# Softmax sums through GpSimd: four key tiles of probabilities added first, values in four column groups

## The reference, cut to what matters

```
x = _group_norm(input, gn_weight, gn_bias)
qkv = jnp.einsum('bchw,oc->bohw', x, qkv_weight)          # q, k, v: 4 heads x 32 channels
attn = jnp.einsum('bnchw,bncyx->bnhwyx', q, k) / math.sqrt(C)
attn = jax.nn.softmax(attn.reshape(B, N_HEAD, H, W, H * W), axis=-1)
out = jnp.einsum('bnhwyx,bncyx->bnchw', attn, v)
out = jnp.einsum('bchw,oc->bohw', out, out_weight) + out_bias[:, None, None]
return out + input
```

## Time and profile before

| | |
|---|---|
| median of 3 runs | 394.5 us (392.34 to 397.24) |
| the profiled execution, its own time | 393.55 us |
| its span, first to last instruction | 391.8 us |
| mean granted clock of PE | 0.916 of full speed |
| busy: PE, DVE, ACT, POOL | 326.7, 222.2, 187.9, 112.0 us |

### The profile page before, as it was taken

One profiled execution on the slowest core, in us unless ns is written; L12 is line 12 of the kernel. 1 busy time (PEld: TensorE's weight loads), 2 busy tenths in 40 slices (PEclk: granted clock), 3 DMA queues, 4 the chain that ended last, 5 costly groups with the idle time before them and its releaser, 6 DMA issues.

```text
span 391.8 us, 6547 instructions
## 1 busy us (share of the span) xinstructions
PE 326.7 (83%) x1970; PEld 208.4 (53%) x1970; DVE 222.2 (57%) x693; ACT 187.9 (48%) x272; POOL 112.0 (29%) x142
## 2 busy tenths in 40 slices
PE   1766739998989989999999878198865998999985
PEld 1433323333433433544524254197865998999985
DVE  2446823456464556264655865376978566888610
ACT  1247115675656665465555511423370465777621
POOL 1086800000000000100011057500371777775420
PEclk9968556999999999999999999869697799999999
DMA  6069495535000000600000001120020214335124
GB/s 183 1 141 228 113 359 119 121 99 212 1 3 1 2 3 27 189 0 2 1 2 0 0 30 47 48 62 22 16 81 8 76 49 125 90 90 160 36 69 173
DMA packets 21773, 29.29 MB, mean 75 GB/s; under 512 B 4055, under 2 KB 15628, under 8 KB 21484
## 3 DMA queue, kind: packets, MB, share of 16 engines
q1 hardware_dynamic: 16828, 18.05, 17.0%
q0 software_dynamic: 3744, 10.31, 8.2%
q10 hardware_dynamic: 1168, 0.52, 0.5%
HBM read 11.62 MB, written 9.25 MB: 53 GB/s over the span
## 4 chain that ended last, share of the span: by engine, by line
PE 57%; DVE 18%; DMA 7%; POOL 7%; issue 6%; SPq 2%; ACT 1%; ACTq 0%; DVEq 0%; POOLq 0%
PE ps L794 13%; PE ps L989 8%; PE ps L977 8%; PE ps L757 6%; POOL expert_in L473 6%; PE ps L775 5%; DVE above L1081 4%; PE ps L737 3%; DMA Qs<-mrow 2%; SPq L331 2%; DMA Qs<-q_hi 2%; DVE pm L1084 2%; DMA attn<-in_L_conv_qkv_weight 1%; PE ps L859 1%; PE ps L693 1%
## 5 line engine op out<-in xcount | busy, mean ns | idle before, releaser
L536 ACT ACTIVATE probs<-ps 128x1024 f32<-128x1024 f32 x64 | 65.3, 1022 | 43.4 <-PE ps L775 43.4
L794 PE MATMUL ps<-probs,vT 128*32 128x512 f32 x256 | 69.2, 617 | 0.1
L794 PE MATMUL ps<-probs,ones 128*32 128x512 f32 x256 | 69.2, 617 | 0.0
L1081 DVE CUSTOM_DVE_ANT_0 above<-ps,above 128x512 f32<-128x512 f32 x56 | 38.7, 691 | 50.3 <-PE ps L757 49.0
L416 POOL TENSOR_TENSOR rstd<-ve,minus_half 128x8 f32<-128x8 f32 (+1 forms) x8 | 11.1, 1385 | 191.5 <-DVE ve L1120 175.2
L989 PE MATMUL ps<-w,GT 128*128 x368 | 52.8, 289 | 7.9 <-ACT GT L637 7.3
L637 ACT ACTIVATE GT<-H 128x512 f32<-128x512 f32 x46 | 29.0, 631 | 57.4 <-DVE H L1342 57.2
L989 PEld LDWEIGHTS ps<-w,GT 128*128 128x128 f32 x368 | 48.0, 204 | 9.6 <-issue 9.5
L977 PE MATMUL ps<-XTT,w1s 128*128 128x128 f32 x368 | 52.4, 289 | 0.0
L529 ACT ACTIVATE above<-ps 128x512 f32<-128x512 f32 x56 | 33.5, 599 | 38.5 <-PE ps L737 38.5
L478 POOL DMA_INDIRECT token_out<-Y,yidx x46 | 44.1, 959 | 22.1 <-DVE Y L1353 14.3
(11 more groups left out here) (185 smaller groups left out, 426.1 us busy)
## 6 DMA issues: line engine op xcount, KB each, us to landing
expert_in<-zeros POOLq DMA_DIRECT2D x2, 1495.0 KB, 8.1
XR<-expert_in SPq DMA_DIRECT2D x46, 65.0 KB, 1.9
Qs<-q_hi SPq DMA_DIRECT2D x16, 128.0 KB, 3.4
w<-in_L_ffn_W SPq DMA_DIRECT2D x1, 2048.0 KB, 8.2
w<-in_L_ffn_W SPq DMA_DIRECT2D x8, 256.0 KB, 4.5
YG<-token_out SPq DMA_DIRECT2D x8, 256.0 KB, 4.2
Ks<-k_hi SPq DMA_DIRECT2D x14, 128.0 KB, 3.1
X<-in_x SPq DMA_DIRECT2D x2, 512.0 KB, 5.0
```

Of the source, the lines that this page charges most:

```text
L536: nc.scalar.activation(probs[:, s % 3, :], bank(2 + 2 * (s % 2), 2), ACT.Exp).then_inc(exp_done, 1)
L794: last = nc.tensor.matmul(bank(6 + o % 2)[i * HD:(i + 1) * HD, :], w, probs[:, s % 3, hd * HALF:(hd + 1) * HALF], start=kt == 0, stop=kt = ...
L1081: nc.vector.tensor_tensor_reduce(above[:, n % 2, :], bank(base), above[:, n % 2, :], scale=1.0, scalar=-3.0e38, op0=ALU.add, op1=ALU.max, ...
```

## The change

The sums over the keys no longer come from PE in every step.

- POOL adds the probabilities of four key tiles (`add_probs`, L504 of the changed kernel): steps 4q to 4q + 3 are quad q, three adds of 128x1024 float32 each, into one of three buffers that lie in X, t2 and X2 of image 1. Of the last quad only the first two steps are added.
- PE multiplies ones with the two quad sums of a group (`sums_of`, L864), in step 8(o + 1) + 1, after the values of that step; for the last group after step 63, with four parts: two quad sums and the probabilities of steps 62 and 63 themselves.
- The product with v (`values`, L845) is cut by head and by query half of the 512 (256 queries each), and so fills the four column groups with 256 columns each. The sums lie in columns 256 to 511 of the same bank.
- There are five buffers of probabilities (`probs_of`): two lie over k_hi and k_lo of image 0 in the first half and over the stacks of image 0 in the second. An exponential waits for the product and the add that read its buffer five steps before; that of step 3 also for the stack DMAs out of k_hi and k_lo.
- The close of a group on DVE is a step later (`s % KT == 2`), waits for the sums too, and works on 128 partitions x 256 columns for the transposes and on 64 x 256 twice for the product.
- "project" moves from step 34 to 35, "tokens_stats tokens" from 35 to 36. The three `rsqrt` of image 0 stand between POOL's adds: after the third add of quad 8 (step 35), the second of quad 12 (step 50), and the first of quad 13 (step 53). The row numbers of image 1 are written after the first scatter.

```diff
+            probs_a, o = at("probs_a", [P, NPR - 3, 2 * HALF], f32, hl_at + 4 * 2 * L)
+            probs_b, o = at("probs_b", [P, NPR - 3, 2 * HALF], f32, stack_at + 4224)
+        def probs_of(s):
+            r = s % NPR
+            if r < 3:
+                return probs[:, r, :]
+            return (probs_a if s < UNITS * STEPS // B else probs_b)[:, r - 3, :]
+
+        def quad_sum(q):
+            return (X[:, 1, :], t2[:, 1, :, :].rearrange("p j c -> p (j c)"),
+                    X2[:, 1, :, :].rearrange("p j c -> p (j c)")[:, 0:L])[q % 3]
...
-        LAYER1_AT = {BEGIN_LAYER1: "residual", 34: "project", 35: "tokens_stats tokens", 39: "keys",
+        LAYER1_AT = {BEGIN_LAYER1: "residual", 35: "project", 36: "tokens_stats tokens", 39: "keys",
...
+        NORMS_AT = {(8, 3): 0, (12, 2): 1, (13, 1): 2}
+        LAST_QUAD = UNITS * STEPS - 4
+        def added_by(s):
+            return 3 * (s // 4) + max(1, s % 4) if s < LAST_QUAD + 2 else 3 * (QUADS - 1) + 1
+        def query_span(o, i):
+            return bank(6 + o % 2)[64 * i:64 * i + 64, 0:QSPAN]
...
+            def add_probs(q, i):
+                s = 4 * q + i
+                pool.wait_ge(exp_done, s + 1)
+                if i == 1 and q >= 3:
+                    pool.wait_ge(sum_done, (q - 3) // 2 + 1)
+                if i > 1:
+                    pool.wait_ge(probs_added, added_by(s - 1))
+                nc.gpsimd.tensor_tensor(quad_sum(q), probs_of(s - 1) if i == 1 else quad_sum(q), probs_of(s),
+                                        ALU.add).then_inc(probs_added, 1)
+            row_numbers(0)
+            pool.wait_ge(resid_ready, B)
+            for q in range(QUADS):
+                for i in range(1, 4 if q < QUADS - 1 else 2):
+                    add_probs(q, i)
+                    if (q, i) in NORMS_AT:
+                        rsqrt(B + NORMS_AT[q, i])
...
-            rsqrt(B)
-            rsqrt(B + 1)
-            rsqrt(B + 2)
             scatter(0, lambda j: rsqrt(B + 3) if j == 3 else None)
+            pool.wait_ge(sum_done, 2 * UNITS)
+            row_numbers(1)
...
-                if s >= 3:
-                    act.wait_ge(pv_done, s - 2)
-                nc.scalar.activation(probs[:, s % 3, :], bank(2 + 2 * (s % 2), 2), ACT.Exp).then_inc(exp_done, 1)
+                if s == 3:
+                    act.wait_ge(stack_in[0], 16 * (6 + SP_LOADS))
+                    act.wait_ge(stack_in_pool, 16 * (6 - SP_LOADS))
+                    act.wait_ge(stack_in[1], 16 * 12)
+                if s >= NPR:
+                    act.wait_ge(pv_done, s - NPR + 1)
+                    act.wait_ge(probs_added, added_by(s - NPR))
+                nc.scalar.activation(probs_of(s), bank(2 + 2 * (s % 2), 2), ACT.Exp).then_inc(exp_done, 1)
...
-                for i, w in ((hd, vT[:, b, kt, n * HD:(n + 1) * HD]), (2 + hd, ones[:, 0:HD])):
-                    last = nc.tensor.matmul(bank(6 + o % 2)[i * HD:(i + 1) * HD, :], w,
-                                            probs[:, s % 3, hd * HALF:(hd + 1) * HALF],
-                                            start=kt == 0, stop=kt == KT - 1)
+                for i in range(2):
+                    for hd in range(2):
+                        n = head(u, hd)
+                        last = nc.tensor.matmul(query_span(o, i)[hd * HD:(hd + 1) * HD, :],
+                                                vT[:, b, kt, n * HD:(n + 1) * HD],
+                                                probs_of(s)[:, hd * HALF + i * QSPAN:hd * HALF + (i + 1) * QSPAN],
+                                                start=kt == 0, stop=kt == KT - 1)
+                last.then_inc(pv_done, 1)
+
+            def sums_of(o):
+                parts = [quad_sum(2 * o), quad_sum(2 * o + 1)]
+                if o < 2 * UNITS - 1:
+                    pe.wait_ge(probs_added, added_by(KT * o + KT - 1))
+                else:
+                    pe.wait_ge(probs_added, added_by(LAST_QUAD))
+                    parts += [probs_of(LAST_QUAD + 2), probs_of(LAST_QUAD + 3)]
+                if o >= 2:
+                    pe.wait_ge(o_used, o - 1)
+                for n, part in enumerate(parts):
+                    for i in range(2):
+                        for hd in range(2):
+                            r = (2 * i + hd) * HD
+                            last = nc.tensor.matmul(bank(6 + o % 2)[r:r + HD, QSPAN:2 * QSPAN], ones[:, 0:HD],
+                                                    part[:, hd * HALF + i * QSPAN:hd * HALF + (i + 1) * QSPAN],
+                                                    start=n == 0, stop=n == len(parts) - 1)
+                last.then_inc(sum_done, 1)
...
+                values(s)
+                if s % KT == 1 and s > KT:
+                    sums_of(s // KT - 1)
...
             def norm_sums(o):
                 dve.wait_ge(pv_done, (o + 1) * KT)
+                dve.wait_ge(sum_done, o + 1)
...
-                link(nc.vector.transpose(sums[:, :], bank(6 + o % 2)[64:128, :]))
+                link(nc.vector.transpose(sums, bank(6 + o % 2)[:, QSPAN:2 * QSPAN]))
...
-                nc.vector.tensor_tensor(place, bank(6 + o % 2)[0:64, :].rearrange("c (p j) -> c p j", j=J),
-                                        rec[:, :].rearrange("c (p j) -> c p j", j=J), ALU.mult).then_inc(o_used, 1)
+                for i in range(2):
+                    at_ = qh * 64 + i * 32
+                    last = nc.vector.tensor_tensor(place[:, at_:at_ + 32, :],
+                                                   query_span(o, i).rearrange("c (p j) -> c p j", j=J),
+                                                   rec[64 * i:64 * i + 64, :].rearrange("c (p j) -> c p j", j=J), ALU.mult)
+                last.then_inc(o_used, 1)
...
-                closing = s % KT == 1 and s > KT
+                closing = s % KT == 2 and s > KT
```

More of the change, by code:

```diff
@@ L35, in build_program @@
     FILLERS = 7
+    NPR = 5
+    QUADS = UNITS * 2 * L // P // 4
+    QSPAN = 256
     NBY = 16
@@ L152, in build_program @@
         rec_sums = sb("rec", [P, HALF])
-        rec, sums = rec_sums[0:64, :], rec_sums[64:128, :]
-        rec16 = sb("rec16", [P, HALF // 32])[64:128, :]
+        rec, sums = rec_sums[:, 0:QSPAN], rec_sums[:, QSPAN:2 * QSPAN]
+        rec8 = sb("rec8", [P, QSPAN // 32])
         kneg = sb("kneg", [P, 2])
@@ L934, in _ @@
                 run_parts(layer1, LAYER1_AT, s, 0)
-                for hd in range(2):
-                    values(s // STEPS, s % STEPS, hd)
+                values(s)
+                if s % KT == 1 and s > KT:
+                    sums_of(s // KT - 1)
                 for g in new[1:2]:
```

38 lines of the change are left out of this document (19 added, 19 removed).

## The result

The changed kernel takes **434.2 us** (median of 4 runs, 431.9 to 434.8), the kernel before 395.9 beside it (392.3 to 397.4). The ratio is **1.097** with a 95% interval of 1.088 to 1.106: 10% slower, where 388.1 was forecast and 397 was the top of the range. On another chip one run of it took 456.5 us beside 418.9 for the kernel before, a ratio of 1.09.

What follows compares the result with a forecast made beforehand. Bound: the PE-DVE slot loop and PE in steps 0 to 31, PE and layer 1's links after. -8.2 + 1.8 = -6.4 from 393.55 gives 387.2; the median, 0.95 above, 388.1 us; range 382.5 to 397.

Steps and rivals of the forecast that it cites:

- two-slot step: Steps 0 to 31, a step serving two row-maxima slots: the slot loop over PE and DVE holds it at 2.58 us.
- the slots do not pay for POOL's traffic: Denies a rival: L1081 (now L1152) grows 0.1 us from POOL's SBUF traffic, costing 5 us: 393 us, chance 0.07.
- Steps 0 to 31: First half: 12.5 us gained, 2.6 for sums and 2.4 for closes charged, 0.7 added: 8.2 us less at step 32.
- hidden: POOL's three adds take 7.4 of the 10.3 us of four steps, with five buffers between: no time charged.
- the links of layer 1 keep their length: Steps 32 to 63: links unchanged but less covered; 11.8 us of waits against 10.0 less work, 1.8 us back.
- L833's wait: Steps 32 to 63, PE waiting for F: 7.8 us link, four steps cover 4.6, so 3.2 us.
- L883's: Steps 32 to 63, PE's wait after L877: 7.8 us link, four steps cover 4.6; 3.3 us, 2.1 more.
- the mask's: Step 60, PE's wait for the mask behind a late close and DVE's routing: 3.2 us where 1.07 stood.
- 2 to 3 us: Rival part: DVE instructions with two SBUF inputs or two-port mode collide with adds; 391 us, chance 0.25 shared with the clock.
- the forecast's rival: Clock falls in new waits behind step 32, notably at L833: 3 us, giving 391; chance 0.25 shared with the collisions.
- Adds become the bound: Rival: POOL's adds slow by half, to 3.8 us, and set the pace: 412 us, chance 0.10.
- More is hidden: Rival: second-half waits come out at half size and the closes cost nothing: 380 us, chance 0.11.

Runs made afterwards that it cites:

- e12: e7 with spare products of 0.92 us in PE's pauses, three of them in steps 0 to 31; 397.4 us against 393.9 for the kernel before.
- e7: Changed kernel with real sums, maxima transposed first and split out of PSUM, POOL holding adds until DVE's normalisations are done; 430.5 us against 417.7 before.
- e6: e1 with every product with the values issued twice; 178.5 us for both stretches from first exponential to scatter, total 431.5 against 417.7 before.
- e8: Changed kernel with real adds and every product with the values issued twice; 205.0 us from first exponential to scatter, total 456.2 against 417.7 before.
- e1: Changed kernel with POOL's adds cut to 8 columns, other sums set to 1; 183.6 us from first exponential to scatter, total 432.8 against 417.9 before.
- e3: Kernel before plus 46 POOL adds at the changed kernel's pace, results unread; 192.6 us against 170.1 to the scatter, total 441.4 against 417.9.
- e2: Changed kernel with each add replaced by a POOL power of 13 columns, as long but with hardly any traffic; 429.0 us against 417.9 before.
- e11: Kernel before with seven of eight products cut to 256 columns, old order, no adds; steps 0 to 31 97.2 us against 93.6, total 401.9 against 393.9.
- e15: e14 without the three spare products; 92.3 us for steps 0 to 31, total 419.8 against 417.4 for the kernel before.
- e14: Steps 0 to 31 of e12, steps 32 to 63 of the kernel before; 412.9 us against 417.4 for the kernel before, ratio 0.987.

## Why the prediction was wrong

**What held.** The two-slot step was forecast at 2.58 us and is 2.58. The adds take 2.34 to 2.44 us and one 2.61 (forecast 2.45), and no exponential of the first half waits for one. L1152 is still at 691 ns, so the slots do not pay for POOL's traffic. The product came to 0.57 where 0.50 was taken: a bare step is 1.23 us (183.12 to 184.35), forecast 1.16. Steps 0 to 31 were forecast at 85.4 us and are 85.2 in e12, once nothing is stopped and the clock is held, the two conditions that the forecast did not name. So close a match is in part luck: e12 has another split of the maxima, up to 3.2 us quicker, and 2.8 us of spare work.

**The step that failed** is "hidden", said of the adds: I asked what POOL had to do beside them and how long PE could wait for them, and not who else needs what an add occupies. With it fell "the links of layer 1 keep their length": the rows they rest on the earlier trace rows were taken while POOL stood idle. L833's wait was forecast at 3.2 us and is 8.73, L883's at 3.3 and is 7.14, the mask's at 3.2 and is 5.42. The price of this step is 27.0 us by e7 (206.8 - 179.8), 26.5 by e6 and e8, 23.2 by e1 and 22.5 by e3.

The prediction did have the rule, as part of a rival at "2 to 3 us". It was undersized by three errors. It missed the shortest instructions concerned, L1090 and L1091, of which I had read no row; four of their fourteen were stopped. It scaled with DVE's time on such work ("half of 8.9 us"), when a stop lasts until the add ends, whatever the instruction's own length: 0.17 us became 2.20. And it took L1125 as one row of 2.14 us, when it is eight instructions, each of which can meet an add anew. The Trainium skill, "SBUF — State Buffer", "Who interferes with whom", states it outright for a VectorE instruction in a two-port mode: the pair of ports that it shares with GpSimd goes to whoever issues first, for the whole instruction, and the other fully blocks. This page I had not weighed. The trace agrees that L1161 is stopped for the rest of the add, all or nothing (2.20 us for 0.17). It does not agree on "for the whole instruction" on POOL's side: e2's instruction of 2.42 us with 13 columns let DVE pass in 0.21.

**The clock** is the second cause, and the forecast's rival put it in the wrong place: in the new waits of the second half, at 3 us. It falls already in steps 0 to 31, at the closes, which stood in the profile before with pauses of 0.8 to 0.9 us at full clock. The shorter product does it: e11, in the old order, without adds, loses all of the gain and 3.6 us more. The measured price in steps 0 to 31 is 7.6 us (e7 against e12), and 5.4 of the 7.2 between e15 and e14. So the clock takes back nearly all of the 8.2 us forecast by itself.

**The sum.** Ahead of the scatter the changed kernel is 206.8 - 163.7 = 43.1 us over the forecast: 27.0 of meetings (with what e7's split gives), 7.4 in steps 0 to 31, which e12 puts down to the clock, and 8.7 behind step 32. Of these 8.7, 6.1 us of meetings are left in e7 on DVE and its clock is .85. Which part each has was not measured; e12 raised the clock only to .92, without gain. In the changed kernel the two causes are not independent: the stops at the maxima rows are pauses of PE too, of 1.77, 2.12, 2.10 and 2.51 us. What they do to its clock is small in the mean of steps 0 to 31: .74 with them and .78 in e1 without.

**The other rivals.** "Adds become the bound" did not happen in the changed kernel, where the adds stayed at 2.4 us: the kernel did become slower, but not by that mechanism. "More is hidden" had nothing for it.

## What to carry to other kernels

Work moved to GpSimd is not free because GpSimd is idle: list every VectorE instruction in that stretch of the kinds that were stopped here (tensor with scalar from SBUF to SBUF, two tensor operands in SBUF), short ones first, and charge each up to a whole GpSimd instruction. Then move them to read PSUM, or order them against each other with a wait. Reductions, transposes and reciprocals kept their length here. A saving on TensorE must be checked against the clock: where it makes the engine arrive early at a pause, a spare matmul of the pause's length can be worth more than the saving. And where one half of a loop is bound by a chain of short links and the other by the step, make the change only in the half where it pays.
